# Three mixes placed side by side and a 64-row MLP chunk stacked to 128 rows, in a transformer block followed by graph attention

## The reference

```python
# layer 0: block with conditioned norms
mods = silu(c) @ adaln_w + adaln_b
x_mod = rms(x) * (1 + scale_msa) + shift_msa
q, k, v = split(x_mod @ qkv_w, 3)                 # 16 heads of 16
q, k = rope(rms(q) * lnq_w, rms(k) * lnk_w)
attn = softmax(q @ k.T / 4) @ v
x = x + gate_msa * (attn @ proj_w + proj_b)
h = rms(x) * (1 + scale_mlp) + shift_mlp
x = x + gate_mlp * ((silu(h @ w1) * (h @ w3)) @ w2)   # hidden width 704 = 5 * 128 + 64
# layer 1: graph attention over the first 20 rows, in two directions
self_feat = concat(x, q_exp) @ W_self.T + b_self
for d in (0, 1):
    aff = where(edge_count > 0, qh @ kh.T / 4, NEG) + (A @ w_bias + b_bias)
    out += (softmax(aff) @ kv) @ Wout[d] + bout[d]
return x + relu(out)
```

## Time and profile before

| | before |
|---|---|
| median of three runs | 1407.96 us |
| the profiled execution | 1400.84 us |
| its span | 1398.9 us |
| PE busy | 1334.7 us (95%) |
| PE weight loads busy | 1228.6 us (88%) |
| DVE busy | 1161.8 us (83%) |
| ACT busy | 888.6 us (64%) |
| POOL busy | 719.1 us (51%) |
| mean granted TensorE clock | 0.977 |
| DMA | 40 GB/s over the span |

### The profile page before, as it was taken

One profiled execution on the slowest core, in us unless ns is written; L12 is line 12 of the kernel. 1 busy time (PEld: TensorE's weight loads), 2 busy tenths in 40 slices (PEclk: granted clock), 3 DMA queues, 4 the chain that ended last, 5 costly groups with the idle time before them and its releaser, 6 DMA issues. The chain is left out here.

```text
span 1398.9 us, 51521 instructions
## 1 busy us (share of the span) xinstructions
PE 1334.7 (95%) x20276; PEld 1228.6 (88%) x20276; DVE 1161.8 (83%) x2065; ACT 888.6 (64%) x1784; POOL 719.1 (51%) x676
## 2 busy tenths in 40 slices
PE   4589999999999999999999999999999999999986
PEld 3579999999999999999999999999999999999875
DVE  5669888888888888888988888898888888888753
ACT  4557666666766666676666667666667667666542
POOL 0245655555565555456555546555555655555441
PEclk9689999999999999999999999999999999999997
DMA  7001111100011110011111001111100111110100
GB/s 243 29 24 31 46 43 43 43 28 25 33 43 43 43 43 18 33 35 43 43 43 43 15 32 39 43 43 43 43 15 28 43 43 43 43 43 8 30 22 9
DMA packets 49827, 56.19 MB, mean 40 GB/s; under 512 B 4352, under 2 KB 47744, under 8 KB 49792
## 3 DMA queue, kind: packets, MB, share of 16 engines
q1 hardware_dynamic: 48944, 53.86, 12.3%
q10 hardware_dynamic: 848, 1.84, 0.4%
HBM read 47.03 MB, written 8.65 MB: 40 GB/s over the span
## 5 line engine op out<-in xcount | busy, mean ns | idle before, releaser
L1318 POOL TENSOR_TENSOR gl<-gf,gh 128x512 fp32r<-128x512 f32 x96 | 124.2, 1294 | 261.6 <-ACT gh L926 261.6
L486 PE MATMUL psum<-nh,w_lo 128*128 128x256 f32 x704 | 182.7, 289 | 0.0
L486 PE MATMUL psum<-nh,w_hi 128*128 128x256 f32 x704 | 177.7, 284 | 0.0
L1318 POOL TENSOR_TENSOR nl<-xn,nh 128x512 fp32r<-128x512 f32 x64 | 98.3, 1536 | 123.2 <-ACT nh L864 123.2
L486 PEld LDWEIGHTS psum<-nh,w_lo 128*128 128x128 f32 x704 | 133.9, 190 | 0.2 <-issue 0.2
L486 PEld LDWEIGHTS psum<-nh,w_hi 128*128 128x128 f32 x704 | 133.2, 189 | 0.0
L1384 POOL TENSOR_TENSOR e<-e,inv 128x640 f32<-128x640 f32 x64 | 82.0, 1282 | 89.2 <-DVE inv L1274 89.2
L486 PE MATMUL psum<-nl,w_hi 128*128 128x256 f32 x704 | 115.5, 282 | 0.0
L926 ACT ACTIVATE gh<-gf 128x512 fp32r<-128x512 f32 x96 | 60.3, 628 | 61.7 <-DVE gf L1202 60.9
L486 PEld LDWEIGHTS psum<-nl,w_hi 128*128 128x128 f32 x704 | 98.0, 188 | 0.0
L486 PE MATMUL psum<-qkv_lo,nh 128*128 128x512 f32 (+1 forms) x256 | 87.8, 354 | 2.8 <-ACT nh L864 2.8
(11 more groups left out here) (186 smaller groups left out, 4414.0 us busy)
## 6 DMA issues: line engine op xcount, KB each, us to landing
adj<-in_adj SPq DMA_DIRECT2D x32, 440.0 KB, 3.4
x_in<-in_x SPq DMA_DIRECT2D x32, 256.0 KB, 2.7
xn<-in_xT SPq DMA_DIRECT2D x32, 256.0 KB, 3.5
x_res<-in_xT SPq DMA_DIRECT2D x32, 256.0 KB, 3.6
out_T<-y SPq DMA_DIRECT2D x32, 256.0 KB, 2.2
e<-in_adaln ACTq DMA_DIRECT2D x2, 512.0 KB, 5.2
stage<-in_qkv SPq DMA_DIRECT2D x2, 384.0 KB, 5.6
pT<-in_w SPq DMA_DIRECT2D x2, 384.0 KB, 7.1
```

The lines of the kernel that those rows point to most:

```text
L486: last = nc.tensor.matmul(out, lhsT, rhs, start=start and i == 0, stop=stop and i == len(terms) - 1)
L1318: return nc.gpsimd.tensor_tensor(out, full, hi.bitcast(F32), ALU.subtract)
```

## The change

The constants `BANK` and `ORDER`, and the code of a few steps, change in five ways:

1. **Stack.** `w2` holds its last 64 rows twice, in partitions 0 to 63 and 64 to 127 of chunk 5. A new ACT step `half_high` copies the high part of the last 64 gate values into partitions 0 to 63 of `gl`'s chunk 5, behind POOL's `gl`. The stacked chunk is then high above low, and mlp_down ends with low and high weights by it at 128 rows: two matmuls for each half of the output, not three. PE waits for `half_hi` ahead of them.
2. **Mixes.** On PE mix 1 of block 2 moves from before qkv 1 to behind mlp_up 2, and mix1 0 with it, so that mix 1, mix1 0 and mix1 1 follow one another. On DVE its normalisation moves behind the gate of mlp_up 2. `pT1` gets a buffer for each tile, so that ACT's copy for tile 1 no longer waits for mix1 0.
3. **Values.** ACT's step qkv is split: squares stay, the copies of v (`values`) are steps of their own; those of tile 1 stand last in the list and wait for mix 1 of the block before.
4. **Self split and edge counts.** ACT's self_split moves ahead of norm1_mean and keys. DVE's edges (L1224) moves from behind mix1 to behind the gate of mlp_up 1.
5. **Banks.** The second half of probsT 1 goes to bank 7 in place of 0, mix 1 to bank 2 in place of 6. The `wait_free` lines follow.

```diff
 BANK = {
-    "xT": 6, "qk": (2, 3), "v": (7, 1), "heads": (7, 5), "probsT": (5, 4, 4, 0), "probsT1": (0, 5, 4, 7),
-    "mix": (5, 6), "q1": (4, 6), "score": 0, "score1": 0, "mixT": 6, "proj": 2, "norm1": 7, "up": (6, 4, 6),
+    "xT": 6, "qk": (2, 3), "v": (7, 1), "heads": (7, 5), "probsT": (5, 4, 4, 7), "probsT1": (0, 5, 4, 7),
+    "mix": (5, 2), "q1": (4, 6), "score": 0, "score1": 0, "mixT": 6, "proj": 2, "norm1": 7, "up": (6, 4, 6),
...
-        (2, "heads", 0), (2, "heads", 1), (0, "self", 0), (1, "norm1_mean", 0), (0, "keys", 0), (0, "self_split", 0),
+        (2, "heads", 0), (2, "heads", 1), (0, "self", 0), (0, "self_split", 0), (1, "norm1_mean", 0), (0, "keys", 0),
...
-        pT0, pT1 = pT[:, 0, :, :], pT[:, 1, :, :]
+        pT0, pT1 = pT[:, 0, :, :], [pT[:, 1, :, :], sb("pT1_1", [P, NJ, P])[:, :, :]]
...
                     elif (t, j) == (1, 4):
-                        wait_free(pe, m, (biased1, -2, 4), (shifted_s, 0, 2))
+                        wait_free(pe, m, (v1_kept, -2, 1), (normed[1], -1, 1), (qkT_kept, 0, 1))
...
+                wait(pe, half_hi, m, 1)
                 for o in both:
-                    for i, (w, a) in enumerate(((wl["w2"], gh), (wh["w2"], gh), (wh["w2"], gl))):
-                        last = nc.tensor.matmul(down_ps[:, o, :], w[half, MC - 1, out_chunks[o]], a[half, MC - 1, :],
-                                                start=False, stop=o == DC - 1 and i == 2, tile_position=(HALF, 0))
+                    last = linear(down_ps[:, o, :], high_terms("w2", out_chunks[o], gl, [MC - 1]), False, o == DC - 1)
...
-                if t == 0:
-                    wait_last(act, mixed, m)
-                v = v_ps.rearrange("p (j h f) -> p j h f", h=2, f=DH)
+
+            def values(m, t):
+                wait(act, qkv_done, m, t + 1)
+                wait(act, mixed, m, t + 1 - TILES)
+                v = qkv_ps[t][1].rearrange("p (j h f) -> p j h f", h=2, f=DH)
...
+            def half_high(m, n):
+                wait(act, g_lo, m, MC // 2)
+                nc.scalar.activation(gl[0:HALF, MC - 1, :], gf[HALF:, 1, :], ACT.Copy).then_inc(half_hi.sem, 1)
+
...
-                wait(act, mixed1, m, t)
-                nc.scalar.activation(pT1[:, 0:4, :], pT1_out[t][0], ACT.Copy).then_inc(pT1_a.sem, 1)
+                wait(act, mixed1, m, t + 1 - TILES)
+                nc.scalar.activation(pT1[t][:, 0:4, :], pT1_out[t][0], ACT.Copy).then_inc(pT1_a.sem, 1)
...
-        "w2": np.insert(a["L0_cond_w2_w"], [HM - HALF] * HALF, 0, 0),
+        "w2": np.concatenate([a["L0_cond_w2_w"], a["L0_cond_w2_w"][HM - HALF:]], 0),
```

More of the change, by code:

```diff
@@ L84 @@
         (3, "norm0_apply", 0), (0, "score1", 0), (0, "v1", 0), (2, "mix", 0), (2, "probsT", 1), (1, "mlp_up", 0),
-        (1, "mlp_up", 1), (3, "qkv", 0), (0, "probsT1", 0), (2, "mix", 1), (3, "qkv", 1), (0, "mix1", 0),
-        (0, "probsT1", 1), (1, "mlp_up", 2), (0, "mix1", 1), (1, "mlp_down", 0), (1, "mlp_down", 1), (2, "mixT", 0),
+        (1, "mlp_up", 1), (3, "qkv", 0), (0, "probsT1", 0), (3, "qkv", 1), (0, "probsT1", 1), (1, "mlp_up", 2),
+        (2, "mix", 1), (0, "mix1", 0), (0, "mix1", 1), (1, "mlp_down", 0), (1, "mlp_down", 1), (2, "mixT", 0),
         (3, "heads", 0),
@@ L95 @@
         (0, "soft1_inverse", 0), (1, "mlp_up", 0), (0, "score1", 1), (0, "soft1", 1), (0, "soft1_inverse", 1),
-        (1, "mlp_up", 1), (2, "mix", 1), (3, "qkv", 0), (3, "qkv", 1), (1, "mlp_up", 2), (0, "mix1", 0),
-        (1, "edges", 0), (3, "rope_scale", 0), (0, "out", 0),
+        (1, "mlp_up", 1), (1, "edges", 0), (3, "qkv", 0), (3, "qkv", 1), (1, "mlp_up", 2), (2, "mix", 1), (0, "mix1", 0),
+        (3, "rope_scale", 0), (0, "out", 0),
     ],
     "Activation": [
-        (2, "rope_scale", 0), (0, "mlp_split", 2), (1, "mixT", 0), (0, "x2_split", 0),
-        (2, "heads", 0), (2, "heads", 1), (0, "self", 0), (1, "norm1_mean", 0), (0, "keys", 0), (0, "self_split", 0),
+        (2, "rope_scale", 0), (0, "mlp_split", 2), (0, "half_high", 0), (1, "mixT", 0), (0, "x2_split", 0),
+        (2, "heads", 0), (2, "heads", 1), (0, "self", 0), (0, "self_split", 0), (1, "norm1_mean", 0), (0, "keys", 0),
         (3, "norm0_mean", 0), (2, "score", 0), (0, "q1", 0), (0, "q1", 1), (2, "probsT", 0), (2, "score", 1),
@@ L104 @@
         (2, "probsT", 1), (1, "mlp_up", 0), (1, "mlp_split", 0), (0, "score1", 1), (1, "mlp_up", 1),
-        (0, "probsT1", 0), (3, "qkv", 0), (1, "mlp_split", 1), (3, "qkv", 1), (0, "probsT1", 1), (1, "mlp_up", 2),
+        (0, "probsT1", 0), (3, "qkv", 0), (3, "values", 0), (1, "mlp_split", 1), (0, "probsT1", 1), (3, "qkv", 1),
+        (1, "mlp_up", 2), (3, "values", 1),
     ],
@@ L638, in proj @@
                 wait(pe, mixed_hi, m, 1)
-                wait_free(pe, m, (cos_part, 1, 1), (biased1, -2, 4))
+                wait_free(pe, m, (mix_normed, 0, 2))
                 for o in both:
@@ L676, in mlp_down @@
                 first_use(m, "w2")
-                half = slice(HALF, P)
                 if n == 0:
@@ L986, in probs_t1 @@
                 wait(act, pT1_ps, m, 2 * t + 1)
-                wait(act, mixed1, m, t)
-                nc.scalar.activation(pT1[:, 0:4, :], pT1_out[t][0], ACT.Copy).then_inc(pT1_a.sem, 1)
+                wait(act, mixed1, m, t + 1 - TILES)
+                nc.scalar.activation(pT1[t][:, 0:4, :], pT1_out[t][0], ACT.Copy).then_inc(pT1_a.sem, 1)
                 wait(act, pT1_ps, m, 2 * t + 2)
-                nc.scalar.activation(pT1[:, 4:8, :], pT1_out[t][1], ACT.Copy).then_inc(pT1_b.sem, 1)
+                nc.scalar.activation(pT1[t][:, 4:8, :], pT1_out[t][1], ACT.Copy).then_inc(pT1_b.sem, 1)
             run_steps(act, "Activation", {
                 "norm0_mean": norm0_mean, "norm1_mean": norm1_mean, "norm0_apply": norm_apply(0),
-                "norm1_apply": norm_apply(1), "qkv": qkv, "rope_scale": rope_scale, "heads": heads, "score": score, "probsT": probs_t, "mixT": mix_t,
-                "mlp_up": mlp_up, "mlp_split": mlp_split, "x2_split": x2_split, "self": self_feat, "self_split": self_split, "keys": keys, "q1": q1, "v1": v1,
+                "norm1_apply": norm_apply(1), "qkv": qkv, "values": values, "rope_scale": rope_scale, "heads": heads, "score": score, "probsT": probs_t, "mixT": mix_t,
+                "mlp_up": mlp_up, "mlp_split": mlp_split, "half_high": half_high, "x2_split": x2_split, "self": self_feat, "self_split": self_split, "keys": keys, "q1": q1, "v1": v1,
                 "score1": score1, "probsT1": probs_t1, "edges": edges,
```

18 lines of the change are left out of this document (9 added, 9 removed).

## The result

The changed kernel takes 1394.54 us (median of 14 runs, 1388.84 to 1402.21), where the kernel before, run again with it, takes 1405.34 (median of 14, 1401.33 to 1409.63). The ratio is 0.9922, with a 95% interval of 0.9902 to 0.9942: 11 us faster, where 26 were forecast. The time lies inside the stated range of 1369 to 1400, but the gain is less than half of the forecast one. The profiled execution took 1389.84 us, its span is 1387.6.

The account below looks back on a forecast made before the run. The prediction took PE, busy 40.80 of 40.93 us a block, to bound the kernel. Its terms summed to 0.86 us a block, 26 us over some 30 blocks, taking the median from 1407.96 to 1382 us, range 1369 to 1400.

Parts of the forecast that it names:

- the sum: Gains and losses of PE's time added per block: 0.58 + 0.42 + 0.18 + 0.21 - 0.23 - 0.3 = 0.86 us of 40.93.
- new chain: End of mlp_down: PE waits for half_high behind ACT's values 1, table load and POOL's gl; loss 0.3, bounds 0.1 and 0.5.
- DVE holds the start of the block: Rival, chance 0.08: DVE's queue from scores to first gate loses PE's net 0.16; gain 0.7 a block, 21 us, 1387.
- the period of 40.1: Sign of being right: one block of the loop takes 40.1 us in the new trace.
- signs of being right: mixT 0.72 behind the gl pair, mixes 2.6 to 2.8, no q1 0 gap, probsT 1 0.85, waits at qkv 1 and half_high.
- Stack, 0.58: End of mlp_down on PE: fewer matmuls and no change of tiling, 0.72 in place of 1.30; gain 0.58, bounds 0.24 and 0.58.
- Mixes, 0.42: Mix 1 and both mix1 in a row on PE save entering and leaving narrow tilings; gain 0.42, bounds 0 and 0.7.
- Self split, 0.18: q1 0's low products on PE lose a 0.28 wait, some 0.1 lost again at norm1_apply; gain 0.18, bounds 0 and 0.28.
- Bank, 0.21: Second half of probsT 1 no longer waits for DVE's biases, 0.85 in place of 1.06; gain 0.21, bounds 0 and 0.21.
- the wait at qkv 1, -0.23: PE at qkv 1, without mix 1 in front, waits for DVE's second gate to free its bank; loss 0.23.
- the slower rival: Chance 0.06: the table load costs a second 1.29 on the chain; PE loses 0.43 a block, 13 us slower, 1421.
- the chain is longer by half a us: Rival, chance 0.17: POOL's low part, ACT's shifted copy or DVE's gate is slower; gain 0.36 a block, 11 us, 1397.

Follow-up runs that it names:

- e3: The kernel before with the stack alone (four 128-row matmuls, half_high): block 40.96 us, run 1404.22 us, ratio 1.0024 to the kernel before.
- e10: The kernel of e8 with DVE's out (y) moved ahead of rope_scale: block 39.91 us, run 1374.78 us, ratio 0.9793 to the kernel before.
- e11: The kernel of e10 without the stack (six 64-row matmuls, no half_high): block 40.30 us, run 1384.83 us, ratio 0.9870 to the kernel before.
- e2: The changed kernel without the stack (six 64-row matmuls, no half_high): block 40.54 us, run 1391.25 us, ratio 0.9915 to the kernel before.
- e9: The kernel before with only ACT's self_split moved ahead of norm1_mean and keys: block 40.65 us, run 1394.95 us, ratio 0.9928.
- e5: The changed kernel with ACT's self_split back behind norm1_mean and keys: block 40.83 us, run 1404.07 us, ratio 0.9988 to the kernel before.
- e6: The changed kernel with the second half of probsT 1 back in bank 0: block 40.52 us, run 1392.01 us, ratio 0.9908 to the kernel before.
- e7: The changed kernel with ACT's qkv 1 squares ahead of mlp_split 1 and probsT1 1, DVE's mix1 and out ahead of mix 1: block 40.30 us, run 1390.27 us.
- e12: The changed kernel with DVE's edge counts back between mix1 and rope_scale: block 41.08 us, run 1408.25 us, ratio 1.0035 to the kernel before.
- e1: The changed kernel with DVE's y formed for 8 of 256 columns only: block 40.28 us, run 1388.20 us, ratio 0.9901 to the kernel before.
- e8: The changed kernel with ACT's order of e7 and mlp_split 2 ahead of the table load: block 40.20 us, run 1383.99 us, ratio 0.9853.

## Why the prediction was right or wrong

The direction and the two waits were right, the size was not: 0.44 a block in place of 0.86. The step that failed is the sum itself, "what is worth something is therefore what PE does or waits for", and in it the last sentence on the new chain: "DVE then has mix 1 and mix1 behind the gate but no edge counts, and comes to rope no later than before". That sentence holds as far as it goes, since DVE came to the gating of x2 0.42 earlier. It was not enough: PE had come 0.72 earlier, the gating stands behind rope on DVE, and the block goes by the gating. That a PE busy for 40.80 of 40.93 us was not alone in setting the block is shown by e3: 0.3 less at mlp_down moved nothing. The prediction had this as a rival only for the start of the block ("DVE holds the start of the block"); it held the end.

As an account of PE's work up to mixT the sum was nearly right. Counted from k1 in the two kernels, PE gained 0.31 by self split, 0.21 by the bank and 0.40 by the mixes, lost 0.30 at qkv 1, gained some 0.56 at the end of mlp_down and lost 0.46 there to the wait: 0.72 of the 0.86. Of that, 0.28 was lost again behind mixT, since DVE came late to the gating. Apart from the period of 40.1, all that the prediction had named as signs of being right came true as well. They could not tell, since each of them is about PE, and none lies behind mixT.

Term by term:

- *Stack, 0.58*: PE's work did go, 0.51 where nothing waits (e10 and e11); the 1.30 of the rows before also held some 0.08 of waiting for POOL's `gl`, which the term counted as changes of tiling. But its worth was 0.00 on the kernel before and 0.02 in the changed one (e3, e2), and 0.39 once DVE's queue was shorter (e11).
- *Mixes, 0.42*: counted from k1 and as means over the middle of the changed kernel, mix 1 starts at 26.60, the two mix1 at 27.66 and the matmul behind them at 29.02: 2.42 in all, where 1.06 + 0.74 + 0.74 = 2.54 was reckoned. From the start of probsT1 0 to that matmul PE takes 8.97 before and 8.87 after with the 0.30 of wait at qkv 1 in it: 0.40 gained. It was not run alone.
- *Self split, 0.18*: 0.31, alone (e9) and in the change (e5). The 0.28 of PE's wait was right, the 0.1 taken off was wrong, since DVE's `x_sq` is no longer held by POOL.
- *Bank, 0.21, and the wait at qkv 1, -0.23*: the first was 0.21, the second 0.30; the block doesn't see the bank (e6), since qkv 1 starts with the second gate in either case.
- *New chain, -0.3*: its length was right to 0.02 (6.42 for 6.4), and PE's wait was 0.46, within the bounds of 0.1 and 0.5, as PE was quicker at the inner borders of the mixes. It did not set the block: e7 has the same mixT as the changed kernel and a block 0.22 shorter.
- *The table load*: it took 1.28 to 1.29 on the chain, and `qk_root` started 0.01 behind it (669.51); the slower rival did not come about. The second part that the Trainium skill adds to a load (ScalarE: Activation LUTs, What ACT_TABLE_LOAD costs) appears in no row here either.
- *Missing altogether*: the length of DVE's instructions. I took each from its row as if it went with the instruction. The rows of before had the sign of it: the first `qr` pair 1.34, the second 0.75.

One rival has the measured number, "the chain is longer by half a us" with 11 us. That is chance: the chain was as long as reckoned, POOL's part 1.30 and `half_high` 0.41.

DVE's 0.42 is made up as follows, in the means over the loop's middle: 0.31 from self split, and another 0.2 by which the gate of mlp_up 2 comes earlier; the edge counts take 0.98 less behind it, mix 1's normalisation 0.63 more, and `y` 0.42 more. The block's 0.44 is 0.31 from self split, shown; 0.02 from the stack and 0.00 from the bank, shown; and some 0.1 from mixes, values and edge counts together, which no run takes apart. Without the move of the edge counts the whole change, self split included, makes the block longer than before (e12). A further 0.24 is regained when `y` is not held (e1, e7), shown. The gain of e8 to e10 over this is of the same kind: e8 takes PE's wait away and leaves DVE waiting for `qk_root`, and e10 fills that wait with `y`, which brings the gating 0.28 and the block 0.29 earlier.

## What to carry to other kernels

With several engines nearly full, look for the instruction behind whose start the rest of the block always takes the same time (here the gating of x2, 6.33 us), and ask which of its inputs comes last: a saving on one engine is worth only the slack up to the other. The same four matmuls for six took 0.3 to 0.5 us a block off PE and were worth nothing, and then 0.39, according to one queue next to it. Reorder a second engine's list also by what runs beside each instruction, and look for instructions of one form with two durations.
